# Graph attention layer and routed expert layer on one core: where the first-layer expert weights are kept, and how the table of steps is worked out

## The reference

```python
h = layernorm(x) @ W.T + b_W
e = leaky_relu((h @ a1)[:, None] + (h @ a2)[None, :] + b_a, 0.2)
x = x + softmax(where(adj > 0, e, -9e15), axis=1) @ h
xf = layernorm(x)
logits = xf @ Wr + br                       # 2048 x 64
topk_logits, topk_idx = top_k(logits, 2)
gates = softmax(topk_logits, axis=1)
for e in range(64):                         # W1[e] 128 x 256, W2[e] 256 x 128
    y = relu(xf @ W1[e] + b1[e]) @ W2[e] + b2[e]
    out = out + combine[:, e:e+1] * y       # combine: the two gates of each row
x = x + out
```

## Time and profile before

| what | us |
|---|---|
| median of three runs | 309.27 |
| the profiled execution, its own time | 310.09 |
| its span, first to last instruction | 308.3 |
| TensorE busy | 228.9 |
| VectorE busy | 216.8 |
| GpSimd busy | 200.0 |
| ScalarE busy | 138.5 |

### The profile page before, as it was taken

How to read it: one execution, slowest core, us unless ns; L and a number is a source line. 1 busy time by engine, 2 the same in 40 slices (tenths; PEclk the granted TensorE clock), 3 DMA queues, 4 the chain that set the end, 5 groups by cost and what they waited for, 6 DMA issues and landing times.

```text
span 308.3 us, 6228 instructions
## 1 busy us (share of the span) xinstructions
PE 228.9 (74%) x1797; PEld 216.3 (70%) x1797; DVE 216.8 (70%) x596; ACT 138.5 (45%) x281; POOL 200.0 (65%) x227
## 2 busy tenths in 40 slices
PE   0692598989958995992823358688799989999850
PEld 0580498889957995991712257577789989999850
DVE  3867999999999999981365615656366757676555
ACT  1126797885965596623033023323253434343310
POOL 5620119989787989888757545465578888886510
PEclk9999699999998999897865558977899999999995
DMA  6884522788986510011101164443546656765057
GB/s 179 151 160 99 87 52 43 219 232 273 274 187 167 224 76 15 6 37 36 52 17 52 40 168 139 112 132 106 136 127 180 182 161 177 188 183 156 28 173 244
DMA packets 26000, 40.62 MB, mean 132 GB/s; under 512 B 3696, under 2 KB 20336, under 8 KB 24944
## 3 DMA queue, kind: packets, MB, share of 16 engines
q1 hardware_dynamic: 20144, 25.14, 27.2%
q0 software_dynamic: 5376, 14.75, 21.1%
q10 hardware_dynamic: 448, 0.33, 0.5%
HBM read 43.32 MB, written 5.28 MB: 158 GB/s over the span
## 4 chain that ended last, share of the span: by engine, by line
PE 42%; DVE 21%; issue 14%; POOL 14%; DMA 6%; another core or an unknown queue 1%; ACT 1%; ACTq 0%; SPq 0%; POOLq 0%; DVEq 0%
PE bank L902 16%; PE bank L912 14%; DVE arena L557 7%; POOL table L360 6%; PE bank L892 2%; POOL ve L340 2%; PE bank L815 2%; DMA arena<-result 2%; DVE arena L542 2%; DMA b_s<-in_b 2%; PE bank L776 2%; POOL nm L345 2%; DVE arena L551 2%; POOL rstd L342 1%; DVE xs L563 1%
## 5 line engine op out<-in xcount | busy, mean ns | idle before, releaser
L902 PE MATMUL bank<-arena 128*128 x380 | 63.8, 293 | 8.3 <-issue 4.4
L815 PE MATMUL bank<-arena 128*128 128x130 f32 x512 | 63.2, 283 | 0.0
L912 PE MATMUL bank<-w2s,arena 128*128 x380 | 61.5, 287 | 1.0 <-issue 1.0
L815 PEld LDWEIGHTS bank<-arena 128*128 128x128 f32 x512 | 62.0, 199 | 0.0
L902 PEld LDWEIGHTS bank<-arena 128*128 128x128 f32 x380 | 53.0, 202 | 11.8 <-issue 11.6
L718 DVE SCALAR_TENSOR_TENSOR arena<-bank,arena 128x128 f32 x95 | 33.2, 350 | 36.1 <-PE bank L912 24.5
L475 ACT ACTIVATE arena<-bank,arena 128x128 f32<-128x128 f32 x95 | 34.9, 367 | 51.6 <-PE bank L902 35.7
L912 PEld LDWEIGHTS bank<-w2s,arena 128*128 128x128 f32 x380 | 53.3, 203 | 1.6 <-issue 1.6
L803 PE MATMUL bank<-ident,arena 128*128 128x128 f32 x256 | 34.2, 291 | 21.4 <-DVE arena L557 21.2
L803 PEld LDWEIGHTS bank<-ident,arena 128*128 128x128 f32 x256 | 30.3, 150 | 24.5 <-DVE arena L557 24.5
L385 POOL DMA_INDIRECT arena<-table,arena x32 | 30.3, 948 | 26.0 <-PE bank L892 16.8
(11 more groups left out here) (155 smaller groups left out, 267.7 us busy)
## 6 DMA issues: line engine op xcount, KB each, us to landing
arena<-in_w1b SPq DMA_DIRECT2D x95, 129.0 KB
arena<-in_adj POOLq DMA_DIRECT2D x16, 512.0 KB, 6.9
w2s<-in_w SPq DMA_DIRECT2D x8, 1024.0 KB
arena<-result SPq DMA_DIRECT2D x4, 512.0 KB, 5.7
xs<-in_x SPq DMA_DIRECT2D x4, 256.0 KB, 5.4
out<-xs SPq DMA_DIRECT2D x4, 256.0 KB, 3.0
table<-rows_out,pos POOLq DMA_INDIRECT x32
arena<-table,arena POOLq DMA_INDIRECT x32
```

The costliest lines, as they stand in the source:

```text
L815: ins = pe.matmul(OB[t % 2][:, 0:D + 2], pt_r[:, t % 2, j, :], h[:, j, :], start=(j == 0), stop=(j == T - 1))
L902: ins = pe.matmul(hp(p, b), w1s[:, p % UW, P * b:P * b + P], xT_all[:, bass.ds(column, P)], start=True, stop=True)
L912: ins = pe.matmul(yp(p), hT[:, p % UH, b, :], w2s[:, bass.ds(e, 1), b, :].rearrange("p e d -> p (e d)"), start=(b == 0), stop=(b == HB - 1))
```

## The change

1. **First-layer weights.** 48 experts' weights (`RING`) are loaded into SBUF whole, in six DMAs of 1 MB: the first needs no room of the attention's, four wait for the last row of scores, the last for the attention's row before its last. `w2s` is a ring of 48 too. The other 16 experts come in four groups of four, 0.5 MB for each layer, when steps 35, 39, 43 and 47 have left the places. SP no longer fetches for each step. Instead ACT copies the step's 128 x 256 weights from the big ring to one of `UW` = 4 tiles that TensorE reads (`fetch`, three steps ahead).
2. **Bias.** `b1` is loaded as it lies (64 x 256) by one more DMA in the first group of small loads, and two matmuls with a table of which step belongs to which expert spread it over the steps (`b1p`).
3. **The table of steps** in closed form: the rounding is done by adding a large constant instead of shifting integers, and the words are packed by matmuls with powers of 32 and 64 in place of a chain on DVE. POOL makes the constants for it at the start (some 25 small instructions more).
4. **Gathers** no longer wait for `e_xt`; the gathered rows land in `rows_out`, whose contents have been written to the table by then.
5. TensorE waits for `s_mask` after its first takes and ups, not ahead of them.

```diff
+            for c in range(RING // HEAD):
+                if c == 1:
+                    sp.wait_ge(s_z, T)
+                if c == RING // HEAD - 1:
+                    sp.wait_ge(s_lk, T - 1)
+                e0 = c * HEAD
+                sp.dma_start(w1s[:, e0:e0 + HEAD, :], w1[:, e0:e0 + HEAD, :]).then_inc(d_w1, 16)
+            for c in range((E - RING) // LATE):
+                e0, u0 = RING + c * LATE, c * LATE
+                done = NB + u0 + LATE - 1
+                sp.wait_ge(e_w, done)
+                sp.dma_start(w1s[:, u0:u0 + LATE, :], w1[:, e0:e0 + LATE, :]).then_inc(d_late1[c], 16)
+                sp.wait_ge(e_y, done)
+                sp.dma_start(w2s[:, u0:u0 + LATE, :, :], w2[:, e0:e0 + LATE, :, :]).then_inc(d_late2[c], 16)
...
-            for p in range(PAIRS):
-                if p >= UW:
-                    sp.wait_ge(e_h, p - UW + 1)
...
-                e = expert_of(sp, experts, p)
-                sp.dma_start(w1s[:, p % UW, :], w1b[:, bass.ds(e, 1), :].rearrange("p e w -> p (e w)")).then_inc(e_w[p % UW], 16)
...
-                if b >= AHEAD:
-                    pool.wait_ge(e_xt, b - AHEAD + 1)
...
+            def fetch(p):
+                if RING <= p < E and (p - RING) % LATE == 0:
+                    act.wait_ge(d_late1[(p - RING) // LATE], 16)
+                if p >= UW:
+                    act.wait_ge(e_h, p - UW + 1)
+                u = slot_of(act, slots, p)
+                act.activation(w1u[:, p % UW, :], w1s[:, bass.ds(u, 1), :].rearrange("p e h -> p (e h)"), ACT.Copy).then_inc(e_w, 1)
...
             for p in range(PAIRS):
                 relu(p)
                 if p + 2 < NB:
                     x_evac(p + 2)
+                if p + UW - 1 < PAIRS:
+                    fetch(p + UW - 1)
...
-            dve.wait_ge(d_small, 16 * 4)
+            dve.wait_ge(d_small, 16 * 5)
...
+            dve.tensor_scalar(mark[:, :], ends, MAGIC, MAGIC + NB - 1, ALU.add, ALU.min).then_inc(s_mark, 1)
...
+            for j in range(PACK):
+                pe.matmul(coded[:, 0:WORDS], radix[:, j:j + 1], r_blk[:, j:TAB:PACK], start=(j == 0), stop=(j == PACK - 1))
```

More of the change, by code:

```diff
@@ L4, with build @@
 from concourse import mybir
-def build(nc, x, adj, weights, biases, w1b, w2, b2, out):
+def build(nc, x, adj, weights, biases, w1, b1, w2, b2, out):
     F32, BF16, I32, U32 = mybir.dt.float32, mybir.dt.bfloat16, mybir.dt.int32, mybir.dt.uint32
@@ L27, in build @@
     CB = 4
-    W1W = HID + HB
     ROW = D + 2
@@ L155, in build @@
         OB, M0, M1 = bank[4:6], bank[6], bank[7]
+        ends, coded, sides, b1_at = bank[0][0:E, 0:2], bank[4][0:1, 0:2 * WORDS], bank[5], bank[3][:, 0:HB * TAB]
         d_x = [sem(f"d_x{i}") for i in range(4)]
         d_small = sem("d_small")
+        d_w1 = sem("d_w1")
         d_w2 = sem("d_w2")
+        d_late1 = [sem(f"d_late1_{i}") for i in range((E - RING) // LATE)]
+        d_late2 = [sem(f"d_late2_{i}") for i in range((E - RING) // LATE)]
         d_adj = [sem(f"d_adj{i}") for i in range(4)]
@@ L220, in build @@
         e_g = [sem(f"e_g{i}") for i in range(UG)]
-        e_w = [sem(f"e_w{i}") for i in range(UW)]
+        e_w = sem("e_w")
         e_xt = sem("e_xt")
@@ L467, in _ @@
                                ident[:, :].rearrange("p (b d) -> p b d", b=1).to_broadcast([P, 16, D]), ACT.Copy, scale=0.0).then_inc(s_zero, 1)
+            act.wait_ge(s_tp, 6)
+            act.activation(b1p[:, :, :], b1_at.rearrange("p (b i) -> p b i", b=HB), ACT.Copy).then_inc(s_b1, 1)
             def x_evac(b):
@@ L650, in _ @@
                         place(q)
-            c_e, o_e, end_e = (edge[:, k:k + 1] for k in range(3))
-            n_e, p_e, pend_e, w_e = (tiles[:, k:k + 1] for k in range(4))
-            u_e = span[:, 1:2]
+            c_e, side_e, w_e = (num[:, k:k + 1] for k in range(3))
+            first_e, last_e = mark[:, 0:1], mark[:, 1:2]
+            dve.wait_ge(s_tri, 1)
             dve.wait_ge(s_tp, 1)
-            dve.tensor_copy(c_e, M0[0:E, 0:1]).then_inc(s_edge, 1)
+            dve.tensor_scalar(edge[0:E, :], M0[0:E, 0:1], 1.0 / P, None, ALU.mult).then_inc(s_edge, 1)
@@ L680, in _ @@
             dve.wait_ge(s_tp, 4)
[L681 to L683 removed]
+            dve.tensor_copy(words, coded.rearrange("p (k i) -> p k i", k=2)).then_inc(s_tab, 1)
             dve.wait_ge(s_tp, 5)
[L686 removed]
@@ L693, in _ @@
-            top = [least[:, k, :, PACK - 1] for k in range(2)]
-            for j in range(PACK - 2, -1, -1):
-                for k, radix in enumerate((32.0, 64.0)):
-                    into = wsum[:, j % 2, k, :] if j else words[:, k, :]
-                    ins = dve.scalar_tensor_tensor(into, top[k], radix, least[:, k, :, j], ALU.mult, ALU.add)
-                    top[k] = into
-                if j:
-                    link(ins)
-            ins.then_inc(s_tab, 1)
-            dve.scalar_tensor_tensor(lo, blk, float(-P), o_p, ALU.mult, ALU.add)
@@ L703, in _ @@
-            link(dve.scalar_tensor_tensor(hi, blk, float(-P), end_p, ALU.mult, ALU.add))
-            link(dve.tensor_scalar(above, lo, pidx[:, :], None, ALU.is_le))
+            lo, hi = (sides[:, k * P:k * P + TAB] for k in range(2))
+            dve.tensor_scalar(above, lo, pidx[:, :], None, ALU.is_le).then_inc(s_above, 1)
+            dve.wait_ge(s_above, 1)
             dve.scalar_tensor_tensor(mask, hi, pidx[:, :], above, ALU.is_gt, ALU.mult).then_inc(s_mask, 1)
@@ L901, in up @@
                 for b in range(HB):
-                    ins = pe.matmul(hp(p, b), w1s[:, p % UW, P * b:P * b + P], xT_all[:, bass.ds(column, P)], start=True, stop=True)
+                    ins = pe.matmul(hp(p, b), w1u[:, p % UW, P * b:P * b + P], xT_all[:, bass.ds(column, P)], start=True, stop=True)
                 ins.then_inc(e_h, 1)
             def down(p):
-                e = expert_of(pe, experts, p)
+                if RING <= p < E and (p - RING) % LATE == 0:
+                    pe.wait_ge(d_late2[(p - RING) // LATE], 16)
+                u = slot_of(pe, slots, p)
                 pe.wait_ge(e_ha, p + 1)
```

204 lines of the change are left out of this document (124 added, 80 removed).

## The result

The changed kernel takes 330.61 us (median of four runs, 327.0 to 332.3) where the kernel before takes 309.30: a ratio of 1.063, 95% interval 1.055 to 1.071. It is slower by 21 us. The forecast was 295.0, faster by 14. The profiled execution took 330.96 us, its span is 329.2.

What follows compares the result with a forecast made beforehand. It took TensorE's matmuls to bound the steps and POOL's gathers, pausing for TensorE, the stretch before. Ending that stretch 14.3 us earlier, the rest unchanged, gave 309.27 - 14.3 = 295.0 us, range 291 to 303.

Steps and rivals of the forecast that it cites:

- Gathers not held back: Block-turning stretch: gathers run 1.25 us apart, TensorE keeps up and turns block 31 at 214.8, so it ends 14.3 us earlier.
- Late signals stay: Rival, chance 0.24: TensorE's signals stay late while gathers run, at worst 1.75 us a turn; 299 us, bounds 296 to 303.
- Start: Small loads at the kernel's start: a fifth load on the same queue costs +0.7 us, bounds 0 and +1.5.
- POOL's constants: About 25 small POOL instructions ahead of the load of `adj` tile 5: covered by 19 us, so cost nothing.
- loading 48 experts: Weight loads after the last scores: 5 MB take 33 us, in by 160, needed at about 174; cost nothing.
- The table: Table of steps before the first turn: that turn starts near 178.6 with the late start, 1.5 us earlier (0 to 3).
- ACT's copies: ACT's 256-column weight copy in each step: 385 ns, a step of 0.75 us under TensorE's 0.89; cost nothing.
- ACT sets the step: Rival, chance 0.10: copies of 595 ns make a step 1.05 us, 63 steps give +10, so 305 us.
- Slower than before: Rival, chance 0.05: ACT's work with nothing overlapping makes a step 1.14 us, so 311 us.
- Late groups: Later expert weights: copy 48 has 11.6 us for a 0.5 MB load against 6.9 us; cost nothing.
- POOL's scatters: Scatters after the gathers: they start at 212.7, 14.1 us earlier, and are no bound yet.
- The lock: Gather stretch: DVE's two-port operations could block GpSimd's DMA descriptors; not seen in the trace, 9 us worse if it held.

Runs made afterwards that it cites:

- Experiments 3 and 4: On two 310-us chips: the gathers' wait for TensorE removed from the kernel before, 327.80 us (1.054); put back into the kernel after, 311.18 us (1.003).
- before_free: The kernel before with only its gathers' wait for TensorE removed: 295.85, 295.44 and 295.92 us on 297-us chips, 327.80 us (1.054) on the other kind.
- before_pause32: The kernel before without its gathers' wait, GpSimd multiplying a 128x32 tile between two gathers: 307.45 us, ratio 0.989, on a 310-us chip.
- before_pause8: The kernel before without its gathers' wait, with work on a 128x8 tile between two gathers: 305.34 us, ratio 1.024, on a 298-us chip.
- after_pause32: The kernel after with work on a 128x32 tile between two gathers: 309.23 us, ratio 1.037, on a 298-us chip.
- the long pause: The kernel after with GpSimd multiplying a 128x128 tile between two gathers: 317.07 us, ratio 1.024, on a 310-us chip.
- the two shorter ones: The kernel before without its gathers' wait, GpSimd multiplying a 128x64 or 128x32 tile between two gathers: 310.24 us (0.999) and 307.45 us (0.989).

## Why the prediction was wrong

**The failed step** is *Gathers not held back*. Its pace was right, gathers from 174.8 to 213.7 against 172.9 to 211.7, if 2 us late; "TensorE turns block 31 at 214.8" was not: that turn starts at 247.9. That is +33.1 us, and the last 18.8 us, from the last step on, in place of 16.8 are +2.0: together they make up the 35.2 between 295.8, forecast for the profiled execution, and its 330.96. The step's sum asks "Can TensorE keep up?" and adds up TensorE's own work alone: it puts the late signals at nothing and leaves them to a rival.

**Late signals stay** was the right mechanism with the wrong size. It took "TensorE makes its old 49/28 = 1.75 us a turn at worst", so that each signal was as late as before, whatever the gathers did. But those 1.75 us had been measured in bursts of three with a pause behind each, and the pause kept the lateness at 2 us; the wait that made the pause was the one being removed. Experiments 3 and 4 show it: the wait removed alone, +17 us; put back, -20 (each counted from the kernel before on the same chip). The rival's own words held the clue: "the signal 2.65 us late at 165.09" comes while GpSimd scatters into the table, and these scatters stand as close as the gathers. In the kernel before, GpSimd, TensorE and VectorE around it:

```profile
164.31 0.96 POOL L360 DMA_INDIRECT table<-rows_out,pos  x1 [0.30 <-issue]
165.58 0.96 POOL L360 DMA_INDIRECT table<-rows_out,pos  x1 [0.30 <-issue]
166.84 0.96 POOL L360 DMA_INDIRECT table<-rows_out,pos  x1 [0.30 <-issue]
165.44 0.35 PE L875 MATMUL bank<-arena,upto_f 64*64 64x1 f32 x2
167.76 0.15 DVE L659 COPY arena<-bank 64x2 f32<-64x2 f32 x1 [2.67 <-remote]
```

Ten scatters go out 0.30 us apart from 157.8 to 169.4, and the signal of the matmul that ends at 165.79 is used at 167.76, 2.0 us late (the 2.65 are the whole wait). "Against: it was one in some 8 us" took the single late signal for a rare one, where it stood at the end of 8 us without a pause and the gathers were about to go on without one for 40.

**On the other kind of chip** the step was right within 0.3 us for the kernel after, which starts to turn block 31 at 214.6; before_free does at 215.5 to 216.3. There the kernel before needed only 297.1 to 297.3 us, so that before_free's 295.4 to 295.9 is 1.3 to 1.8 better, not 14, and the kernel after's 298.85 is 1.6 worse. The 14.3 us of the forecast were almost wholly late signals of one kind of chip.

**Start**, +0.7: the last small load lands at 8.72 us in place of 8.21, so +0.5; further on it is not told apart from the scatter between executions, where the first gather of the kernel after starts between 173.0 and 174.8 and that of the kernel before and its variants between 172.3 and 173.8. **POOL's constants** and **loading 48 experts**, nothing: right, no wait for either. **The table**, first turn at 178.6: 177.7 in the result and 175.5 on the other kind, against 180.15, better than the term. **ACT's copies**, 385 ns: 409 (95 times, 38.6 us), and hidden: the steps behind the last turn take 62.1 us as before (the 399 that the prediction worked out from the Trainium skill, ScalarE: Activation LUTs, "What ACT_TABLE_LOAD costs", are nearer than my line between two rows), so **ACT sets the step** falls, and **Slower than before**, which I had hung on ACT, came true by another mechanism. **Late groups**: no wait. **POOL's scatters**: no bound in the result; on the other kind they run without a wait until near 265 us, behind TensorE.

**The lock** of DVE and GpSimd did not bite: gathers stay at 0.95 us on both kinds of chip, with DVE busy 10 or 35 of 50 us. But the same section of the Trainium skill (SBUF — State Buffer, "SBUF: two separate sides") says that only the port pair that these two share makes contention and that TensorE never waits for anyone. As far as it speaks of SBUF, no run here contradicts it. Read as "GpSimd's gathers cannot touch TensorE", it is contradicted by the signal that is 28 us late.

**Open:** what differs between the chips, whether signal or write is late, what fills up in the first 8 us and what the pause lets through. **A version that beats both kernels** everywhere was not found. Of those tried, before_free is best on 297-us chips (0.993 to 0.995), before_pause32 on the others (0.989); before_free loses 5% on the other kind. before_pause32 was not run on the other kind; as no signal holds it up where it was run, I estimate that it takes its 307.45 us there too, some 3% more than the kernel before (before_pause8 and after_pause32 took 2.4% and 3.7% more).

## What to carry to other kernels

Ask of a wait that you remove what else it did. Here it paced GpSimd's gathers, and its pauses were what let TensorE's signals pass. A stop that shows in the trace and has no known cause is to be priced as growing with whatever goes on beside it, until a run says otherwise, and the trace is to be read for what stood beside it; and one kernel is to be timed on more than one chip before a few per cent are believed, as the same two programs stood 1.063 to each other on one and 1.003 on another.

## What was not expected of the hardware

The experiments were made on seven chips. On three of them the kernel before took 309.8 to 311.0 us, as in the result (309.3), on four 297.1 to 298.1. No chip was measured at two times, so that it is the chip, and not something that changes from time to time, is likely but not shown.

The difference goes with late signals of TensorE while GpSimd issues indirect transfers 0.4 us or less apart: late by 2.0 to 2.2 us in bursts of three, by up to 29.7 us in an unbroken run of 32, and by 0.4 us at most on the other four chips. It happens beside scatters as well as beside gathers. The signal of TensorE that VectorE waits for during the ten scatters into the table (165.79 to 167.76 us in the kernel before) is late in every profile from a chip of the 310-us kind, nine of nine, by 0.5 to 2.0 us, and in none of the eleven from the other kind (0.04 us). It comes ahead of the gathers, so it tells the chips apart whatever is done between them: the profiles of the long pause and of the two shorter ones, in which the gathers hold up little or nothing, have it too (0.93, 1.98 and 0.61 us). GpSimd's own instructions and the steps behind do not tell the chips apart.
